# A two-layer graph convolution on one Trainium2 core: the summing matmuls of a unit write 64 x 384 blocks in two column groups instead of 32 x 192 blocks in four

## The reference, cut to what matters

```
def gcn_conv(x, edge_index, W, b, n_nodes):     # out = D^-1/2 (A + I) D^-1/2 (x W^T) + b
    ...                                         # loops (j, j) are added to the edges
    norm = dinv[src] * dinv[dst]
    h = x @ W.T
    msg = h[src] * norm[:, None]
    out = segment_sum(msg, dst, n_nodes)
    return out + b

h = maximum(layernorm(x), 0)
x = x + gcn_conv(relu(gcn_conv(h, W1, b1)), W2, b2)
h = maximum(layernorm(x), 0)
x = x + attention(h, ...)                       # 12 heads of 64, softmax over a node's edges
```

## Time and profile before

| | |
|---|---|
| device time, median of 3 runs | 1934.79 us (1933.72 to 1936.58) |
| profiled execution, span from first to last instruction | 2277.0 us |
| busy: TensorE matmul, VectorE, ScalarE, GpSimd | 1621.1, 1121.9, 718.1, 1232.7 us |
| indirect gathers: convolutions, attention | 834, 417 |
| DMA traffic | 585.22 MB |

### The profile page before, as it was taken

One profiled execution on the slowest core, in us unless ns is written; L12 is line 12 of the kernel. 1 busy time (PEld: TensorE's weight loads), 2 busy tenths in 40 slices (PEclk: granted clock), 3 DMA queues, 4 the chain that ended last, 5 costly groups with the idle time before them and its releaser, 6 DMA issues. The chain is left out here.

```text
span 2277.0 us, 43588 instructions
## 1 busy us (share of the span) xinstructions
PE 1621.1 (71%) x13579; PEld 962.8 (42%) x13580; DVE 1121.9 (49%) x2027; ACT 718.1 (32%) x2184; POOL 1232.7 (54%) x1297
## 2 busy tenths in 40 slices
PE   7337888887778858787788887882666666666665
PEld 7223444444344424344444444671334444444443
DVE  6613334333334314444444444653666666666666
ACT  6400111111111101000000100262666666777675
POOL 2166566566656266566666666106555555555550
PEclk9969888899988869798988888986787777878877
DMA  4698888888878387788787887388788888888882
GB/s 183 218 315 269 268 266 271 274 265 277 275 264 270 125 279 270 261 270 277 262 274 266 266 275 274 122 310 280 245 279 267 270 267 272 273 273 272 273 276 84
DMA packets 139992, 585.22 MB, mean 257 GB/s; under 512 B 30616, under 2 KB 32752, under 8 KB 139946
## 3 DMA queue, kind: packets, MB, share of 16 engines
q0 software_dynamic: 100272, 497.49, 65.7%
q1 hardware_dynamic: 32563, 67.72, 8.6%
q10 hardware_dynamic: 7110, 19.43, 2.2%
HBM read 534.42 MB, written 50.12 MB: 257 GB/s over the span
## 5 line engine op out<-in xcount | busy, mean ns | idle before, releaser
L667 POOL DMA_INDIRECT ring_c<-table,slot_c x834 | 798.1, 957 | 545.9 <-issue 268.5
L1243 POOL DMA_INDIRECT ring<-table,slot x417 | 410.4, 984 | 288.5 <-issue 105.8
L833 DVE TENSOR_TENSOR hots<-iota,units 128x256 f32<-128x256 bf16 x102 | 43.3, 426 | 602.4 <-remote 332.9
L1493 PE MATMUL ps_acc<-ring,hot_f 128*32 128x195 f32 x3136 | 230.8, 386 | 138.2 <-issue 84.4
L1388 ACT ACTIVATE ring<-ring,weight x1152 | 281.5, 340 | 0.6
L1651 DVE TENSOR_TENSOR ring<-ring,ps_w 128x3120 f32 x72 | 244.7, 3398 | 16.5 <-issue 8.9
L1493 PEld LDWEIGHTS ps_acc<-ring,hot_f 128*32 128x32 f32 x3136 | 123.9, 125 | 227.7 <-issue 124.2
L808 PE MATMUL ps_ya<-weights,sum_ta 128*128 128x512 f32 (+1 forms) x576 | 204.1, 503 | 12.5 <-issue 10.9
L808 PE MATMUL ps_yb<-weights,sum_tb 128*128 128x512 f32 (+1 forms) x576 | 196.7, 494 | 6.1 <-issue 5.5
L711 ACT ACTIVATE slot_c<-units 128x8 int32 (+1 forms) x104 | 21.7, 211 | 545.9 <-DMA ring_c<-table,slot_c 391.8
L779 PE MATMUL ps_sum0b<-ring_c,hots 128*32 128x192 f32 x1600 | 136.3, 364 | 75.9 <-issue 66.6
(11 more groups left out here) (294 smaller groups left out, 2121.0 us busy)
## 6 DMA issues: line engine op xcount, KB each, us to landing
ring_c<-table,slot_c POOLq DMA_INDIRECT x834
table<-ft SPq DMA_DIRECT2D x25, 396.0 KB, 2.8
table<-nodes SPq DMA_DIRECT2D x25, 384.0 KB
table<-nodes ACTq DMA_DIRECT2D x25, 384.0 KB
turned_table<-h_t SPq DMA_DIRECT2D x25, 384.0 KB, 3.0
nodes<-in_x ACTq DMA_DIRECT2D x24, 384.0 KB
turned_g<-turned_table SPq DMA_DIRECT2D x24, 384.0 KB
out_x<-nodes SPq DMA_DIRECT2D x24, 384.0 KB
```

What stands on the lines that cost most here:

```text
L667: eng.indirect_dma_start(out=ring[:, t * QH + k, :], out_offset=None, in_=table, in_offset=bass.IndirectOffsetOnAxis(ap=slot[t][:, k:k + 1 ...
L833: eng.tensor_tensor(hots[k][:, :, :].rearrange("p (s c) d -> p s c d", c=CPU), iota0[:, :].unsqueeze(1).unsqueeze(2).to_broadcast([P, 2, C ...
L1243: eng.indirect_dma_start(out=ring[:, b * RB + at * FROW:b * RB + (at + 1) * FROW], out_offset=None, in_=table3, in_offset=bass.IndirectOff ...
L1493: last = eng.matmul(acc_of(s, g), hot_f[:, c, s * UD:(s + 1) * UD], ring[:, x0 + g * GW:x0 + (g + 1) * GW], start=False, stop=True, skip_g ...
```

## The change

A pair of units (0 and 1, or 2 and 3) shares one block of 64 destinations. The one-hot of a chunk is now 64 columns wide, and the half that belongs to the other unit is zero: `pair_hots[h]` has three slots of 32 columns for each chunk, the middle one zeroed once, and `hot_of` takes slots 0 and 1 for the even unit and slots 1 and 2 for the odd unit. A chunk is then two matmuls of 384 columns, each writing 64 partitions, instead of four of 192 writing 32. `ps_sum` has another layout, 64 destinations x 384 features in each of four blocks; the addition of `natural` takes 4 instructions instead of 16, and the transposes 8 instead of 2. In the first convolution VectorE zeroes both `pair_hots` at its start.

```
+UP = US // 2
+PW = 2 * UD
+GP = P // PW
+GC = D // GP
...
-        hots = [sb(by_conv, f"hots{k}", [P, n, UD]) for k, n in enumerate((2 * CPU, 2 * CPU, US))]
+        pair_hots = [sb(by_conv, f"pair_hots{h}", [P, CPU, 3, UD]) for h in range(UP)]
+        extra_hot = sb(by_conv, "extra_hot", [P, US, UD])
...
-                def block_of(par, s, g):
-                    c0 = (s // 2) * 512 + (s % 2) * GB
-                    return ps_sum[par][g * UD:(g + 1) * UD, c0:c0 + GB]
+                def block_of(par, h, g):
+                    return ps_sum[par][g * PW:(g + 1) * PW, h * 512:h * 512 + GC]
+
+                def hot_of(s, c):
+                    return pair_hots[s // 2][:, c, s % 2:s % 2 + 2, :].rearrange("p x d -> p (x d)")
...
-                            for g in range(US):
-                                last = eng.matmul(block_of(par, s, g), hot, rows[:, g * GB:(g + 1) * GB], start=start, stop=True, skip_group_check=True)
+                            for g in range(GP):
+                                last = eng.matmul(block_of(par, s // 2, g), hot, rows[:, g * GC:(g + 1) * GC], start=False, stop=True, skip_group_check=True)
...
-                                            last = add(par, s, hots[s // 2][:, (s % 2) * CPU + c, :], ring[:, s * CPU + c, :])
+                                            last = add(par, s, hot_of(s, c), ring[:, s * CPU + c, :])
...
+                            for h in range(UP):
+                                eng.memset(pair_hots[h][:, :, :, :], 0.0).then_inc(s_blank, 1)
+                            eng.wait_ge(s_blank, UP)
                             eng.sem_inc(s_b, 1)
...
-                                for s in range(units_of(j)):
-                                    for g in range(US):
-                                        block_ = block_of(par, s, g)
-                                        last = eng.tensor_tensor(block_, block_, natural[s * UD:(s + 1) * UD, g * GB:(g + 1) * GB], ALU.add)
+                                for h in range(-(-units_of(j) // 2)):
+                                    for g in range(GP):
+                                        block_ = block_of(par, h, g)
+                                        last = eng.tensor_tensor(block_, block_, natural[h * PW:(h + 1) * PW, g * GC:(g + 1) * GC], ALU.add)
...
-                                for b in range(2):
-                                    last = eng.transpose(turned(j)[:, :, b * 2 * UD:(b + 1) * 2 * UD].rearrange("p k (s d) -> p s k d", d=UD),
-                                                         ps_sum[par][:, b * 512:b * 512 + 2 * GB].rearrange("p (s k d) -> p s k d", s=2, d=UD))
+                                for g in range(GP):
+                                    for f in range(2):
+                                        for s in range(2):
+                                            to, of = (g * 2 + f) * UD, (g * 2 + s) * UD
+                                            last = eng.transpose(turned(j)[to:to + UD, :, :].rearrange("p k (h s d) -> p h s k d", h=UP, d=UD)[:, :, s],
+                                                                 ps_sum[par][of:of + UD, :].rearrange("p (h x) -> p h x", h=UP)[:, :, f * GB:(f + 1) * GB].rearrange("p h (k d) -> p h k d", d=UD))
```

More of the change, by code:

```diff
@@ L638, in convolution @@
                 s_pre = sem(st, f"s_pre{tag}")
-                s_bn = sem(st, f"s_bn{tag}")
+                s_blank, s_bn = (sem(st, f"s_blank{tag}"), None) if first else (None, sem(st, f"s_bn{tag}"))
                 def node(j):
@@ L770, in _ @@
                             for b in range(2):
-                                last = eng.matmul(ps_sum[par][:, b * 512:b * 512 + 2 * GB], ident[:, :], nodes[:, 0, 0:2 * GB], start=True, stop=True)
+                                last = eng.matmul(ps_sum[par][:, b * 512:b * 512 + GC], ident[:, :], nodes[:, 0, 0:GC], start=True, stop=True)
                         last.then_inc(s_y, 1)
@@ L775, in _, with add @@
                         last.then_inc(s_nat, 1)
-                        def add(par, s, hot, rows, start=False):
-                            for g in range(US):
-                                last = eng.matmul(block_of(par, s, g), hot, rows[:, g * GB:(g + 1) * GB], start=start, stop=True, skip_group_check=True)
+                        def add(par, s, hot, rows):
+                            for g in range(GP):
+                                last = eng.matmul(block_of(par, s // 2, g), hot, rows[:, g * GC:(g + 1) * GC], start=False, stop=True, skip_group_check=True)
                             return last
@@ L797, in visit @@
                                     for c0, n in HALVES:
-                                        last = eng.matmul(ps_x[:, c0:c0 + n], hots[2][:, :, :].rearrange("p s d -> p (s d)"), ring[:, QX, c0:c0 + n], start=False, stop=True, skip_group_check=True)
+                                        last = eng.matmul(ps_x[:, c0:c0 + n], extra_hot[:, :, :].rearrange("p s d -> p (s d)"), ring[:, QX, c0:c0 + n], start=False, stop=True, skip_group_check=True)
                                     last.then_inc(extra_done, 1)
@@ L817, in _ @@
                         else:
+                            for h in range(UP):
+                                eng.memset(pair_hots[h][:, :, :, :], 0.0).then_inc(s_blank, 1)
+                            eng.wait_ge(s_blank, UP)
                             eng.sem_inc(s_b, 1)
                         def clear(par):
-                            eng.memset(ps_sum[par][:, :].rearrange("p (b c) -> p b c", b=2)[:, :, 0:2 * GB], 0.0).then_inc(s_clear, 1)
+                            eng.memset(ps_sum[par][:, :].rearrange("p (b c) -> p b c", b=2)[:, :, 0:GC], 0.0).then_inc(s_clear, 1)
                         eng.wait_ge(s_y, 1)
@@ L832, in next_hot @@
                                 of = dl[:, 2 * k:2 * k + 2, 0:CPU].unsqueeze(3).to_broadcast([P, 2, CPU, UD])
-                                eng.tensor_tensor(hots[k][:, :, :].rearrange("p (s c) d -> p s c d", c=CPU), iota0[:, :].unsqueeze(1).unsqueeze(2).to_broadcast([P, 2, CPU, UD]),
+                                eng.tensor_tensor(pair_hots[k][:, :, 0:3:2, :].rearrange("p c s d -> p s c d"), iota0[:, :].unsqueeze(1).unsqueeze(2).to_broadcast([P, 2, CPU, UD]),
                                                   of, ALU.is_equal).then_inc(hot_ready[k], 1)
                             else:
-                                eng.tensor_tensor(hots[2][:, :, :], iota0[:, :].unsqueeze(1).to_broadcast([P, US, UD]),
+                                eng.tensor_tensor(extra_hot[:, :, :], iota0[:, :].unsqueeze(1).to_broadcast([P, US, UD]),
                                                   dl[:, :, CPU].unsqueeze(2).to_broadcast([P, US, UD]), ALU.is_equal).then_inc(hot_ready[2], 1)
```

## The result

The changed kernel took 1937.95 us (median of 10 runs, 1934.32 to 1940.98) beside 1934.26 us for the kernel before (10 runs, 1930.56 to 1937.67): a ratio of 1.0030, 95% interval 1.0018 to 1.0042. The forecast was 1943 us, slower by 0.4%. The sign and the size came out, and so did the place; one step of the reasoning, what the slow stretches of TensorE are, did not.

What follows compares the result with a forecast made beforehand. GpSimd's gathers, 21.3 us a tile, were taken to bound the kernel. The bulk added 0 us and the two convolution ends 3.9 us each, so 1934.8 + 7.8 gave about 1943 us; range 1893 to 1985.

Steps and rivals of the forecast that it cites:

- The bulk is at the pace of the gathers: Convolutions: unprofiled runs go nearly everywhere at the pace of GpSimd's gathers, 17 a tile, 21.3 us.
- A chunk of 0.645 us: Summing matmuls: after the change two groups run beside each other, 0.322 us a pass, 0.645 us a chunk instead of 0.33.
- The 250 us of array time are hidden: Convolution bulk: TensorE's tile grows to 19.6 us, under 21.3 us of gathers, 1.7 us to spare, so 0 us.
- rival 2: Convolution tiles: at a granted clock of 0.86 TensorE becomes the bound, 22.8 us a tile, +73 us, 2016 us; chance 0.15.
- VectorE: Additions and transposes in each tile: net -0.5 us a tile, hidden in the bulk, worth nothing by itself.
- 1 us of cover: End of convolution b: last transposes end at 1455, the last product starts at 1456.2, so their extra time costs 0.
- up to 2 us an end: Last transposes at a convolution's end: the cost allowed if a VectorE instruction is dearer than worked out.
- The ends: After each convolution's last gather nothing covers TensorE: 1.3 plus 2.6 us, 3.9 us each, 7.8 us together.
- unit 3: Tile 23, near each convolution's end: it ends 1.3 us later and pushes everything behind it.
- The slow stretches are mostly the profiler's: TensorE in the convolutions: 342 us of the 2277.0 us profiled span do not exist without the profiler.
- Rival 1: TensorE's slow feeding is in unprofiled runs too; fewer records make the kernel faster, 1860 or 1902 us; chance 0.28.

Runs made afterwards that it cites:

- condition A: Occasions on which the unchanged kernel before took medians of 1931 to 1935 us, steadily, whichever kernels ran beside it.
- condition B: Occasions on which the unchanged kernel before took medians of 2287 to 2312 us, steadily, whichever kernels ran beside it.
- the trace with the tiny matmuls: Kernel before plus 96 tiny bf16 matmuls ahead of the product of 22 tiles in each convolution: ratio 1.0039, on an occasion with the shorter times.
- the second: Changed kernel, unchanged, compared again with the kernel before: 1940.83 us against 1930.85, ratio 1.0051.

## Why the prediction was right, and where it was wrong

- *The bulk is at the pace of the gathers.* Right for the runs of condition A: GpSimd's waits in the convolutions are 30 us, where the profile of B had 262, and 416 gaps of 1.25 us are 520 us of the 531 that a convolution takes.
- *A chunk of 0.645 us.* Right: two records beside each other, mean 503 ns, a unit of 2.8 us with the tail. "TensorEngine Tiling (Array Packing)" in the Trainium skill, section "Overview", gives up to two times for 64 columns and up to four for 32; by that rule the chunk is 0.645 us, and the trace agrees.
- *The 250 us of array time are hidden.* Right in A, with 1.6 us a tile to spare in the one looked at where 1.7 was worked out, 1.4 on average over 44 tiles, and with hardly a wait of GpSimd for a unit (the row names 1.8 us). The clock, on which rival 2 hung, was 0.98 over the convolutions, where the trace with the tiny matmuls, the only one of the old form in A, has 0.89.
- *VectorE.* The additions cost 567 ns (564 worked out), the transposes 579, more than the 525 taken and the 562 of the bound. In the bulk it moved nothing in A, and at the end of convolution a the last transposes still end before the last product starts. At the end of convolution b, the place for which the forecast had worked out 1 us of cover, they don't: the last product starts 0.5 us late in both traces of the changed kernel, within the "up to 2 us an end" that was given.
- *The ends.* The right place, with 7.8 us for 4.9 to 5.3 in the traces. Two terms were mis-sized, one at each end. In convolution a it is the last tile's units: 2.6 us worked out, 1.6 measured, since TensorE had waited 0.72 us for rows before. In convolution b it is unit 3: 1.3 us later worked out, 1.4 earlier measured, since the unit had run at half clock in the trace of the old form. With only one trace of the old ends in A, whether that unit always does is open. That the sum came near the time owes something to luck. The time moved by 3.7 us between the medians of the first comparison (5.8 by the ratio) and by 10 in the second; the ends account for about 5 of it, and what the rest of the 10 is stays open.
- *The slow stretches are mostly the profiler's.* Wrong as it stands. This step took two numbers of different conditions, 2277 and 1935, for one kernel with and without a profiler. In B all timed runs take about what the profiled one takes; in A the profiled runs are as short as the others (spans of 1938.9, 1935.1 and 1936.8 us). A run's time is 1.8 us more than its span in both. Whether recording has a part in B at all stays open, by the two reservations above. "Runtime: NRT & Kernel Launch" in the Trainium skill, section "The ~15µs preamble/postamble breakdown", says that a profile's total time exceeds the time that the runtime reports by some 6 us whatever the kernel. That is another pair of numbers than the span and the time here, of which the time is the longer, so its 6 us can't be compared with the 1.8. What I had drawn from it, that a span is nearly the true time, was the better guide, and I set it aside. What I drew from the step, that the timed runs go at the gathers' pace, held all the same, because these runs were of A.
- *Rival 1, slow feeding in unprofiled runs too, decided faster.* False where the forecast was made for, true in B: -33 us. Had the comparison been made there, the forecast would have been wrong in sign, and 1.6% is what the rival gave for half of the waits (1902 us, 1.7% under 1935).

The cause of condition B is open. Shown is that it goes with the occasion or the chip and not with the kernel, that it is TensorE's (VectorE, ScalarE and GpSimd keep their busy times), and that the new form of the summing matmuls helps. That it helps by its fewer instructions is an argument and not shown: the form also brings longer records and a higher clock (0.87 over the span against 0.82). Whether the price goes by the instruction, by stretches, or by something else was not told apart.

## What to carry to other kernels

Before weighing an engine's busy time, find what sets the pace of the loop (here 17 gathers of 1.25 us), and work out the engine's whole turn beside it; in condition A doubling the array's work cost only what lies past the last gather, as far as the traces show. The ends of a pipeline, where nothing covers the late engine, deserve their own sum, with the waits that are there now taken off. And when the profiled span and the timed median are far apart, the first question is whether both come from the same condition, and from the same chip: the sign of this change hangs on it.

## What the runs showed that was not expected

The same kernel took 1931 or 2311 us on different occasions and chips, and the change is worth +0.3 to +0.5% in the one and -1.6% in the other. The attention's window was 708 and 581 us with the same instructions. A stream transpose of 32 partitions x 384 elements took 579 ns, one of 128 x 384 562 ns: with the same elements in a partition, a quarter of the partitions saved nothing. In the last unit of tile 23 of convolution b TensorE ran at a granted clock of 0.50 in the old form (with the tiny matmuls), after 2.85 us of waiting, and over the convolutions at 0.89; in the new form it idles less and had 0.98.
